# First stage of a four-stage transformer kernel: a tiled product with stationary tokens recast as seven half-size products with stationary weights

## The chip, the cores and the metric

One core of one Trainium2 chip runs the whole program in one launch. The metric is the device time in microseconds. Three runs of the kernel before gave 2706.06, 2711.64 and 2711.44 us (median 2711.44).

## What is computed

The reference stacks eight audio frames into each token (3008 tokens of 2560 numbers), normalises, applies two linear layers with a gate between them, then attention, a feed-forward layer and residual sums. Only the start concerns the change:

```python
x = _rms_norm(x, ln_pre_w)                 # x: 3008 tokens x 2560
h = jnp.einsum('btd,hd->bth', x, w1)       # w1: 1024 x 2560
d = h.shape[-1] // 2
h = jax.nn.silu(h[..., d:]) * h[..., :d]   # 3008 x 512
y = jnp.einsum('btd,od->bto', h, w2)       # the next stage
return _rms_norm(y, ln_post_w)
```

The root-mean-square factor of a token may be put on after the product, since it is one number per token; the kernel does so.

## The kernel before, in words

The program is a chain of five stages: `tok_up`, `tok_down`, `attention`, `attn_out` and `ffn`. Each is one block in which every engine runs its own list, with semaphores between the lists; the next stage begins when all lists of the one before have ended. The change lies in `tok_up` (line 239), with one load in `tok_down` (line 541).

Every product is made in three passes: each operand is split into a high part, which ScalarE (ACT) makes by a copy to the matmul's float type, and a low part, the remainder, which VectorE (DVE) makes by a subtraction. `three_pass` (line 230) then issues high x low, low x high and high x high into the same sum.

`tok_up` works in 24 tiles of 128 tokens. SyncE (SP) loads each tile twice, in four chunks: transposed (`x_t` into `raw`, line 300) for the product, and by rows (`x_rows` into `xs`, line 309) for the sum of squares. ACT makes `x_hi` (L327) and the squares (L336), DVE makes `x_lo` (L366). TensorE (PE) holds the tokens stationary and streams 512 columns of weights: 20 parts of the contraction x 3 passes x 2 halves = 120 matmuls a tile, 2880 in all (L235). All of `w1` lies split in SBUF; its 40 pieces are loaded, multiplied by the norm's weights `fac` and split during the first tile (L203, L213, L222). ACT then applies silu (L345), DVE multiplies the halves (L374), PE turns the result over in four transposes (L415), ACT copies it out (L350) and SP stores it (L294). The next stage loads it by tile (line 541).

GpSimd (POOL) does nothing in this stage. The order on each engine is written out by hand and repeated for every tile; a step of two stages in depth lets the gate of one tile run beside the product of the next.

## Time and profile before

| | us |
|---|---|
| median of three runs | 2711.44 |
| lowest, highest run | 2706.06, 2711.64 |
| span of the profiled execution | 2708.5 |
| last `tok_up` matmul begins to end | about 695 |
| first load of `tok_down` issued | 700.50 |

The profile gives one execution, from its first to its last instruction; its span stands in for its own time, and it lies 2.9 us below the median of the runs. Rows of groups read: line of the kernel, engine, operation, output<-inputs, shape, count, then busy time in us and the mean of one in ns, then the idle time before them and what ended it. PE is TensorE's matmuls, PEld its loads of the stationary operand, SPq the issue of a DMA by SyncE. [...]

### The profile page before, as it was taken

How to read it: one execution, taken by the hardware profiler on the slowest of the kernel's cores; microseconds unless marked ns; L12 is line 12 of the kernel's file. 1: busy time of each engine (PE TensorE's matmuls, PEld its weight loads, DVE VectorE, ACT ScalarE, POOL GpSimd, SP SyncE). 2: the span in 40 equal slices, each digit the busy share in tenths (PEclk: the TensorE clock that was granted, in tenths of full speed). 3: DMA queues.
4: the chain of work that ended last, by engine and by line, in shares of the span. 5: the costliest groups of instructions: out<-in, count | busy, mean ns of one | idle time of the engine just before them, and what ended most of it. 6: DMA issues, size and time to landing. Idle time of an engine off the chain costs nothing. (4 is left out here: it accounts for less than half of the span.)

```text
span 2708.5 us, 47164 instructions
## 1 busy us (share of the span) xinstructions
PE 2569.8 (95%) x15800; PEld 2242.7 (83%) x15800; DVE 1400.3 (52%) x3285; ACT 1108.6 (41%) x3526; POOL 568.0 (21%) x582
## 2 busy tenths in 40 slices
PE   6999999999699997999999999989999999699998
PEld 4888888888577776899999999868888888699998
DVE  5121221222366665799899899841111111777775
ACT  6222222222344444889899899831111110211010
POOL 0000000000011121666666666600000000111110
PEclk9999999999799998999999999989999999899999
DMA  7323233332444543111111111163332222322121
GB/s 238 125 86 127 86 115 98 101 112 89 161 157 153 181 152 114 50 47 42 45 45 41 45 45 41 41 221 102 104 99 93 93 93 70 108 71 71 62 78 47
DMA packets 157346, 260.59 MB, mean 96 GB/s; under 512 B 16432, under 2 KB 92720, under 8 KB 157232
## 3 DMA queue, kind: packets, MB, share of 16 engines
q1 hardware_dynamic: 150048, 233.63, 26.4%
q0 software_dynamic: 7184, 25.69, 2.6%
q8 instruction: 40, 0.66, 0.1%
q14 instruction: 74, 0.61, 0.1%
HBM read 177.49 MB, written 81.79 MB: 96 GB/s over the span
## 5 line engine op out<-in xcount | busy, mean ns | idle before, releaser
L1137 ACT ACTIVATE attn_prob<-attn_prob,attn_bias 94x94 f32<-94x94 f32 x1024 | 367.3, 361 | 58.1 <-DVE attn_bias L1214 58.0
L366 DVE TENSOR_TENSOR up_x_lo<-up_raw,up_x_hi 128x640 fp32r<-128x640 f32 x96 | 79.2, 825 | 474.7 <-ACT up_x_hi L327 474.6
L235 PE MATMUL up_ps_h<-up_w_hi,up_x_lo 128*128 128x512 f32 x960 | 301.5, 396 | 22.1 <-DVE up_w_lo L222 19.1
L235 PE MATMUL up_ps_h<-up_w_lo,up_x_hi 128*128 128x512 f32 x960 | 298.3, 392 | 0.0
L235 PE MATMUL up_ps_h<-up_w_hi,up_x_hi 128*128 128x512 f32 x960 | 298.1, 392 | 0.0
L1346 DVE TENSOR_TENSOR out_x_lo<-out_raw,out_x_hi 128x512 fp32r<-128x512 f32 x96 | 66.5, 693 | 400.0 <-ACT out_x_hi L1331 399.9
L235 PE MATMUL out_ps_h<-out_w_hi,out_x_lo 128*128 128x512 f32 x768 | 238.6, 392 | 11.4 <-DVE out_w_lo L220 10.8
L1331 ACT ACTIVATE out_x_hi<-out_raw 128x512 fp32r<-128x512 f32 x96 | 60.6, 631 | 433.9 <-PE out_ps_h L235 282.7
L1496 POOL TENSOR_TENSOR ffn_res<-shared_h,ffn_bias 128x1024 f32<-128x1024 f32 x24 | 59.7, 2492 | 850.4 <-DMA ffn_bias<-base_b 555.3
L235 PE MATMUL out_ps_h<-out_w_lo,out_x_hi 128*128 128x512 f32 x768 | 237.3, 390 | 0.0
L235 PE MATMUL out_ps_h<-out_w_hi,out_x_hi 128*128 128x512 f32 x768 | 237.2, 390 | 0.0
L1253 POOL TENSOR_TENSOR attn_prob<-attn_prob,attn_share 94x752 f32<-94x752 f32 x128 | 184.3, 1440 | 219.9 <-DVE attn_share L1222 219.9
L235 PEld LDWEIGHTS up_ps_h<-up_w_hi,up_x_lo 128*128 128x128 f32 x960 | 179.0, 189 | 62.1 <-issue 15.7
L235 PEld LDWEIGHTS up_ps_h<-up_w_hi,up_x_hi 128*128 128x128 f32 x960 | 181.5, 189 | 38.6
L235 PEld LDWEIGHTS up_ps_h<-up_w_lo,up_x_hi 128*128 128x128 f32 x960 | 181.4, 189 | 38.4
L327 ACT ACTIVATE up_x_hi<-up_raw 128x640 fp32r<-128x640 f32 x96 | 71.0, 739 | 330.3 <-PE up_ps_h L235 222.5
L1137 ACT ACTIVATION_READ_ACCUMULATOR attn_prob<-attn_prob,attn_bias 94x1 f32 x1024 | 191.6, 187 | 0.0
L235 PEld LDWEIGHTS out_ps_h<-out_w_hi,out_x_lo 128*128 128x128 f32 x768 | 144.0, 188 | 44.1 <-issue 11.3
L235 PEld LDWEIGHTS out_ps_h<-out_w_lo,out_x_hi 128*128 128x128 f32 x768 | 144.8, 188 | 30.2
L235 PEld LDWEIGHTS out_ps_h<-out_w_hi,out_x_hi 128*128 128x128 f32 x768 | 144.5, 188 | 30.0
L235 PE MATMUL ffn_ps_o<-ffn_w_hi,ffn_xt_lo 128*128 128x390 f32 (+1 forms) x576 | 139.8, 351 | 10.2 <-DVE ffn_xt_lo L1584 10.2
L1193 DVE TENSOR_TENSOR attn_prob<-attn_ps_s,attn_mask 94x752 f32<-94x752 f32 x128 | 119.5, 933 | 56.5 <-PE attn_ps_s L1060 56.2
(206 smaller groups left out, 5373.7 us busy)
## 6 DMA issues: line engine op xcount, KB each, us to landing
up_raw<-x_t SPq DMA_DIRECT2D x96, 320.0 KB, 4.4
up_xs<-x_rows SPq DMA_DIRECT2D x96, 320.0 KB, 3.6
out_raw<-o_t SPq DMA_DIRECT2D x96, 256.0 KB, 4.3
o_t<-attn_o_t SPq DMA_DIRECT2D x128, 188.0 KB, 1.9
shared_ring<-wo SPq DMA_DIRECT2D x32, 512.0 KB, 5.2
y<-down_y POOLq DMA_DIRECT2D x24, 512.0 KB, 3.0
out_y<-y SPq DMA_DIRECT2D x24, 512.0 KB, 5.7
h<-out_h SPq DMA_DIRECT2D x24, 512.0 KB, 3.1
```

What stands on the lines that cost most here:

```text
L235: last = nc.tensor.matmul(o, x, w, start=a, stop=b, skip_group_check=onto)
L327: nc.scalar.activation(x_hi[c][:], raw[c][:], ACT.Copy).then_inc(hi_done, 1)
L366: nc.vector.tensor_tensor(x_lo[c][:], raw[c][:], x_hi[c][:], ALU.subtract).then_inc(lo_done, 1)
L1137: last = nc.scalar.activation(prob[u % NPR][0:SEQ, h, part], prob[u % NPR][0:SEQ, h, part], ACT.Exp, bias=bias[u % 2][0:SEQ, n:n + 1], sca ...
L1193: nc.vector.tensor_tensor(p4, ps_s[0:SEQ, :, 0:GT].rearrange("p h (b k) -> p h b k", b=GB), mask[0:SEQ, :].unsqueeze(1).unsqueeze(1).broad ...
L1253: nc.gpsimd.tensor_tensor(p4, p4, share[u % 2][0:SEQ, :].unsqueeze(2).broadcast_to((SEQ, 8, SEQ)), ALU.mult).then_inc(prob_done, 1)
L1331: nc.scalar.activation(x_hi[c][:], raw[c][:], ACT.Copy).then_inc(hi_done, 1)
L1346: nc.vector.tensor_tensor(x_lo[c][:], raw[c][:], x_hi[c][:], ALU.subtract).then_inc(lo_done, 1)
L1496: nc.gpsimd.tensor_tensor(res[u % 3][:], h[u % 3][:], bias[:], ALU.add).then_inc(res_done, 1)
```

## The change

The product is computed transposed: weights stand in the array, tokens stream past, so the outcome comes out with hidden units on the partitions, as the next stage wants it, and the transposes fall away. The 3008 tokens are cut into six chunks (502, 502, 502, 502, 500, 500), which form three pairs of a left and a right half. The 2560 inputs are cut into two halves of ten parts and the 1024 outputs into two halves of four blocks. Each of these 2x2-by-2x2 products is then made by seven products in place of eight: an operand is one block or the sum or difference of two, and each outcome is added to, set in or subtracted from one or two blocks of the result `c_t`, which lies in SBUF.

The work is 7 products x 3 pairs x 10 parts = 210 steps; one step is 4 blocks x 3 passes = 12 matmuls of 502 (or 500) columns, 2520 in all. For a step SP loads one or two pieces of x (257 KB each); where there are two, POOL adds or subtracts them (`both`, L502); ACT makes the high part `t_hi` (L562) and DVE the low part `t_lo` (L664). There are five buffers of each. For every product ten new pieces of the stationary operand are made: SP loads one or two weight pieces through three slots (`w_raw`, L445), ACT scales the one (L533), DVE adds the other (`w_sum`, L620), ACT makes `s_hi` (L544) and DVE `s_lo` (L609). They are made one each at steps 5 to 10 of the third pair of the product before (and at two steps of the second pair), and the last two at the first two steps of the product itself. At steps 6 to 9 DVE folds the outcomes of the group before from PSUM into `c_t`.

During the first four products ACT also squares each piece of x (L577), and DVE or POOL sums the squares. In the fifth product 24 one-column matmuls sum them over the partitions, DVE takes the inverse root, and before each of three groups PE spreads it over the partitions by two matmuls whose outcome ACT copies out at the group's fifth step (L591). The gate runs over 4 x 502 elements at a time (L696, L700, L705).

Cut to its core:

```diff
-def tok_up(nc, d, split, ident):
+TOKC = [(0, 502), (502, 502), (1004, 502), (1506, 502), (2008, 500), (2508, 500)]
+SEVEN = [
+    Product([(0, 0)], [(0, 1), (1, 1)], [(0, 1, SET)], minus_b=True),
+    Product([(1, 0), (1, 1)], [(0, 0)], [(1, 0, SET), (1, 1, FROM)]),
+    Product([(0, 0), (0, 1)], [(1, 1)], [(0, 1, ADD), (0, 0, NEG)]),
+    Product([(1, 1)], [(1, 0), (0, 0)], [(1, 0, ADD), (0, 0, ADD)], minus_b=True),
+    Product([(0, 0), (1, 1)], [(0, 0), (1, 1)], [(0, 0, ADD), (1, 1, ADD)]),
+    Product([(1, 0), (0, 0)], [(0, 0), (0, 1)], [(1, 1, ADD)], minus_a=True),
+    Product([(0, 1), (1, 1)], [(1, 0), (1, 1)], [(0, 0, ADD)], minus_a=True),
+]
+def tok_up(nc, d, ident):
+    KH = KIN // 2
+    PAIR = 3
+    NS, NT, NR, NWR = KH + 2, 5, 6, 3
...
+        def weights_at(s):
+
+            i, pr, kk = place(s)
+            out = []
+            if i == 0 and pr == 0 and kk + 1 < KH:
+                out.append(kk + 1)
+            if i + 1 < NI:
+                if pr == 1 and kk in (2, 6):
+                    out.append((i + 1) * KH + (kk - 2) // 4)
+                if pr == 2 and kk >= 4:
+                    out.append((i + 1) * KH + kk - 2)
+            if i > 0 and pr == 0 and kk < 2:
+                out.append(i * KH + KH - 2 + kk)
...
+            def load_weights(q):
+                p, kk = SEVEN[q // KH], q % KH
+                for k, (mh, kh) in zip(w_of[q], p.a):
+                    old = w_slots.before(k)
+                    if old is not None:
+                        sp.wait_ge(s_lo_done, old + 1)
+                    sp.dma_start(w_raw[w_slots.slot(k)][:],
+                                 d["w1"][:, KH * kh + kk, HID * mh:HID * mh + HID]).then_inc(w_in[w_slots.slot(k)], 16)
+
+            def load_x(s):
+                i, pr, kk = place(s)
+                for k, (kh, nh) in zip(x_of[s], SEVEN[i].b):
+                    old = raws.before(k)
+                    if old is not None:
+                        if is_sum(old):
+                            sp.wait_ge(both_done, nth_sum[old] + 1)
+                        else:
+                            sp.wait_ge(lo_done, old + 1)
+                        if old in squared:
+                            sp.wait_ge(sq_done, squared.index(old) + 1)
+                    sp.dma_start(raw[raws.slot(k)][:, 0:width(pr)],
...
+            nc.gpsimd.memset(zero[:], 0.0).then_inc(zero_set, 1)
+            for s in range(STEPS):
+                i, pr, kk = place(s)
+                w = width(pr)
+                if is_sum(s):
+                    n = nth_sum[s]
+                    for k in x_of[s]:
+                        pool.wait_ge(raw_in[raws.slot(k)], 16 * raws.uses(k))
+                    if n >= 2:
+                        pool.wait_ge(lo_done, sums[n - 2] + 1)
+                    a, b = (raw[raws.slot(k)][:, 0:w] for k in x_of[s])
+                    nc.gpsimd.tensor_tensor(both[n % 2][:, 0:w], a, b, SEVEN[i].op_b).then_inc(both_done, 1)
...
+            def first_piece(q):
+
+                p, kk = SEVEN[q // KH], q % KH
+                k = w_of[q][-1]
+                mh, kh = p.a[-1]
+                act.wait_ge(w_in[w_slots.slot(k)], 16 * w_slots.uses(k))
+                if len(p.a) == 1:
+                    dst, sem = s_hi[q % NS], s_hi_done
+                    free_slot(q)
+                else:
+                    dst, sem = w_one, one_done
+                    n = nth_w_sum[q]
+                    if n > 0:
+                        act.wait_ge(sum_done, n)
+                at = KH * kh + kk
+                nc.scalar.activation(dst[:], w_raw[w_slots.slot(k)][:], ACT.Copy, scale=fac[:, at:at + 1]).then_inc(sem, 1)
+
+            def free_slot(q):
+                if q >= NS:
+                    i, kk = (q - NS) // KH, (q - NS) % KH
...
+            def second_piece(q):
+                if len(SEVEN[q // KH].a) == 2:
+                    act.wait_ge(sum_done, nth_w_sum[q] + 1)
+                    free_slot(q)
+                    nc.scalar.activation(s_hi[q % NS][:], w_sum[:], ACT.Copy).then_inc(s_hi_done, 1)
...
+            def weights_sum(q):
+                p, kk = SEVEN[q // KH], q % KH
+                if len(p.a) == 2:
+                    k = w_of[q][0]
+                    at = KH * p.a[0][1] + kk
+                    dve.wait_ge(w_in[w_slots.slot(k)], 16 * w_slots.uses(k))
+                    dve.wait_ge(one_done, nth_w_sum[q] + 1)
+                    dve.wait_ge(s_lo_done, q)
+                    nc.vector.scalar_tensor_tensor(w_sum[:], w_raw[w_slots.slot(k)][:], fac[:, at:at + 1], w_one[:],
+                                                   ALU.mult, p.op_a).then_inc(sum_done, 1)
...
+            def take(g, m):
+
+                i, pr = g // PAIR, g % PAIR
+                w = width(pr)
+                dve.wait_ge(used, KH * g + KH)
+                src = ps[g % 2][m][:, 0:w]
+                for mh, nh, how in SEVEN[i].into:
+                    c = c_t[:, MB * mh + m, cols(pr, nh)]
+                    if how != SET and how != NEG:
+                        dve.wait_ge(taken, 4 * (g - PAIR) + m + 1)
+                    if how == SET:
+                        ins = nc.vector.tensor_copy(c, src)
+                    elif how == NEG:
+                        ins = nc.vector.tensor_scalar(c, src, -1.0, None, ALU.mult)
+                    elif how == FROM:
+                        ins = nc.vector.tensor_tensor(c, c_t[:, MB * 0 + m, cols(pr, nh)], src, ALU.subtract)
+                    else:
+                        ins = nc.vector.tensor_tensor(c, c, src, ALU.add)
+                ins.then_inc(taken, 1)
...
+                for m in range(MB):
+                    if kk == 0 and g >= 2:
+                        pe.wait_ge(taken, 4 * (g - 2) + m + 1)
+                    if kk == 0 and g == STAT_AT and m == 3:
+                        pe.wait_ge(stat_taken, 1)
+                    if kk == 0 and g in RATE_AT and m >= 2:
+                        pe.wait_ge(rate_taken, 2 * RATE_AT[g][m - 2] + 2)
+                    o = ps[g % 2][m][:, 0:w]
+                    sh, sl = (x[q % NS][:, P * m:P * m + P] for x in (s_hi, s_lo))
+                    nc.tensor.matmul(o, sh, tl, start=(kk == 0), stop=False)
+                    nc.tensor.matmul(o, sl, th, start=False, stop=False)
+                    last = nc.tensor.matmul(o, sh, th, start=False, stop=(kk == KH - 1))
+                last.then_inc(used, 1)
...
-                    sp.dma_start(g_raw[u % 2][:], d["g_t"][t].rearrange("p (j c) -> p j c", j=4)).then_inc(g_in[u % 2], 16)
+                    sp.dma_start(g_raw[u % 2][:], d["g_t"][:, :, bass.ts(t, P)]).then_inc(g_in[u % 2], 16)
...
-    for n, shape in (("wq_pair", (PAIRS, P, 2, 2 * P)), ("wvo", (P, PAIRS, DM)), ("g_t", (TILES, P, HID)),
+    for n, shape in (("wq_pair", (PAIRS, P, 2, 2 * P)), ("wvo", (P, PAIRS, DM)), ("g_t", (P, 4, TOKP)),
```

How the weights reach the engines, on two lists. First SyncE's list of DMAs in `tok_up`. Before, in the first tile, weight pieces go through five buffers, and each waits for the low part made from the buffer's last piece:

```order
L203 DMA up_gt0<-w1 128x512 [waits split_lo_done]
L203 DMA up_gt1<-w1 128x512 [waits split_lo_done]
L203 DMA up_spare0<-w1 128x512 [waits split_lo_done]
L309 DMA up_xs1<-x_rows 128x640
L300 DMA up_raw0<-x_t 128x640 [waits up_lo_done]
L309 DMA up_xs0<-x_rows 128x640 [waits up_sq_done]
```

After, in the last steps of the fifth product (each of its successor's operands is a sum of two pieces):

```order
L459 DMA up_raw2<-x_f 128x500 [waits up_both_done]
L459 DMA up_raw3<-x_f 128x500 [waits up_both_done]
L445 DMA up_w_raw2<-w1 128x512 [waits up_s_lo_done]
L445 DMA up_w_raw0<-w1 128x512 [waits up_s_lo_done]
L459 DMA up_raw4<-x_f 128x500 [waits up_both_done]
L459 DMA up_raw5<-x_f 128x500 [waits up_both_done]
L445 DMA up_w_raw1<-w1 128x512 [waits up_s_lo_done]
L445 DMA up_w_raw2<-w1 128x512 [waits up_s_lo_done]
```

What moved: the weight pieces now come in pairs through three slots, in the middle of the loads of x, and stay there for six steps in a row before each product and two at its start.

Second, VectorE's list. Before, one tile in the steady part:

```order
L366 TENSOR_TENSOR up_x_lo<-up_raw,up_x_hi 128x640 [waits up_link,up_hi_done]
L366 TENSOR_TENSOR up_x_lo<-up_raw,up_x_hi 128x640 [waits up_hi_done] x3
L374 SCALAR_TENSOR_TENSOR up_sil<-up_ps_h,up_r,up_sil 128x512 [waits up_sil_done]
L379 TENSOR_REDUCE up_var<-up_ssq 128x1 [waits up_sq_done]
L380 TENSOR_SCALAR up_var<-up_var 128x1 [waits up_link]
L130 TENSOR_SCALAR up_var<-up_var 128x1 [waits up_link]
```

After, two steps at the end of the fifth product:

```order
L620 SCALAR_TENSOR_TENSOR up_w_sum<-up_w_raw,up_fac,up_w_one 128x512 [waits up_s_lo_done,up_one_done,up_w_in2]
L640 TENSOR_TENSOR up_c_t<-up_c_t,up_ps_0 128x502 [waits up_taken,up_used]
L640 TENSOR_TENSOR up_c_t<-up_c_t,up_ps_0 128x502 [waits up_taken]
L609 TENSOR_TENSOR up_s_lo<-up_w_sum,up_s_hi 128x512 [waits up_s_hi_done]
L664 TENSOR_TENSOR up_t_lo<-up_both,up_t_hi 128x500 [waits up_hi_done]
L620 SCALAR_TENSOR_TENSOR up_w_sum<-up_w_raw,up_fac,up_w_one 128x512 [waits up_s_lo_done,up_one_done,up_w_in1]
```

What moved: between the sum of two weight pieces and its low part now stand two folds of outcomes into `c_t`, and the low part of the next x piece stands behind all of them.

## Rows read from the trace of the kernel before

**Rows 1.** The page: busy time in us by engine, share of the span, instructions.

```profile
PE 2569.8 (95%) x15800; PEld 2242.7 (83%) x15800; DVE 1400.3 (52%) x3285; ACT 1108.6 (41%) x3526; POOL 568.0 (21%) x582
```

**Rows 2.** Busy time in a stretch: us; per engine busy (instructions); clock, DMA share, GB/s.

```profile
300.00:400.00 100.00, 100.00 (x450) 82.75 (x450) 21.45 (x62) 25.75 (x50) 0.00 (x0) 1.00 0.27 88
```

**Rows 3.** Timeline of PE in the first stage: start us, us, engine, line, operation.

```profile
300.50 0.62 PE L235 MATMUL up_ps_h<-up_w_hi,up_x_lo 128*128 128x512 f32 x2
300.95 0.62 PE L235 MATMUL up_ps_h<-up_w_lo,up_x_hi 128*128 128x512 f32 x2
```

**Rows 4.** Timeline of PE in the second stage, matmuls into one PSUM bank.

```profile
760.84 0.34 PE L235 MATMUL down_ps_a<-down_wa_lo,down_xt_hi 128*128 128x384 f32 x1
761.01 0.34 PE L235 MATMUL down_ps_a<-down_wa_hi,down_xt_hi 128*128 128x384 f32 x1
```

**Rows 5.** Instructions of the silu tile: ns min/median/max, first and last start us.

```profile
L345 ACT ACTIVATE up_sil<-up_ps_h,up_r x24: 669/669/690, 63.3 to 695.2; 128x512 f32<-128x512 f32 x24
```

**Rows 6.** Timeline of all engines at the start of the first stage.

```profile
7.06 1.42 DVE L222 SCALAR_TENSOR_TENSOR up_w_lo<-up_sil,up_fac,up_w_hi 128x512 fp32r<-128x512 f32 x2 [0.17 <-ACT up_w_hi L213]
7.83 0.99 SPq L203 DMA_DIRECT2D up_sil<-w  x2
8.62 1.19 PE L235 MATMUL up_ps_h<-up_w_hi,up_x_lo 128*128 128x512 f32 x2 [8.62 <-DVE up_w_lo L222]
10.45 0.72 ACT L213 ACTIVATE up_w_hi<-up_sil,up_fac 128x512 fp32r<-128x512 f32 x1 [0.83 <-DMA up_sil<-w]
```

**Rows 7.** Timeline at the end of the first stage and the start of the second.

```profile
694.55 0.61 PE L235 MATMUL up_ps_h<-up_w_hi,up_x_hi 128*128 128x512 f32 x2
698.04 0.35 SPq L294 DMA_DIRECT2D g_t<-up_gt  x1
700.50 0.34 SPq L541 DMA_DIRECT2D down_g_raw<-g_t  x1
703.41 0.63 ACT L654 ACTIVATE down_g_hi<-down_g_raw 128x512 fp32r<-128x512 f32 x1 [5.39 <-DMA down_g_raw<-g_t]
```

**Rows 8.** Groups by line: ACT's and DVE's prices, then POOL's.

```profile
L213 ACT ACTIVATE up_w_hi<-up_sil,up_fac 128x512 fp32r<-128x512 f32 x16 | 11.2, 722 | 5.7 <-DMA up_sil<-w 5.6
L222 DVE SCALAR_TENSOR_TENSOR up_w_lo<-up_sil,up_fac,up_w_hi 128x512 fp32r<-128x512 f32 x16 | 11.6, 748 | 4.8 <-ACT up_w_hi L213 4.7
L1346 DVE TENSOR_TENSOR out_x_lo<-out_raw,out_x_hi 128x512 fp32r<-128x512 f32 x96 | 66.5, 693 | 400.0 <-ACT out_x_hi L1331 399.9
L732 DVE TENSOR_TENSOR down_xt_lo<-down_ps_x,down_xt_hi 128x512 fp32r<-128x512 f32 x48 | 30.8, 680 | 0.4 <-ACT down_xt_hi L647 0.4
L1240 POOL TENSOR_TENSOR attn_by_sin<-attn_swapped,attn_sin 128x376 f32<-128x376 f32 x128 | 125.9, 984 | 7.4 <-DVE attn_swapped L1173 7.4
L1496 POOL TENSOR_TENSOR ffn_res<-shared_h,ffn_bias 128x1024 f32<-128x1024 f32 x24 | 59.7, 2492 | 850.4 <-DMA ffn_bias<-base_b 555.3 <-DVE ffn_o L1618 295.1
L1156 DVE TENSOR_TENSOR attn_w_lo<-attn_w_raw,attn_w_hi 128x256 fp32r<-128x256 f32 x32 | 54.8, 1714 | 0.0
```

**Rows 9.** Timeline of POOL and DVE in the attention stage.

```profile
1400.51 1.44 POOL L1253 TENSOR_TENSOR attn_prob<-attn_prob,attn_share 94x752 f32<-94x752 f32 x1 [1.64 <-DVE attn_share L1222]
1401.91 0.98 POOL L1240 TENSOR_TENSOR attn_by_sin<-attn_swapped,attn_sin 128x376 f32<-128x376 f32 x1
...
1401.39 1.79 DVE L1156 TENSOR_TENSOR attn_w_lo<-attn_w_raw,attn_w_hi 128x256 fp32r<-128x256 f32 x1
```

**Rows 10.** Busy time in stretches, columns as in rows 2 (PE, PEld, DVE, ACT, POOL).

```profile
10.00:20.00 10.00, 7.90 (x28) 5.72 (x26) 5.99 (x9) 6.99 (x11) 0.00 (x0) 1.00 0.91 297
30.00:40.00 10.00, 7.50 (x26) 5.62 (x25) 7.76 (x11) 6.91 (x11) 0.00 (x0) 0.83 0.80 253
705.00:730.00 25.00, 14.02 (x39) 10.54 (x40) 15.67 (x30) 13.37 (x20) 1.74 (x2) 0.65 0.82 270
```

**Rows 11.** The page's DMA issues: count, KB each, median us to landing.

```profile
up_sil<-w SPq DMA_DIRECT2D x16, 256.0 KB, 4.1
out_raw<-o_t SPq DMA_DIRECT2D x96, 256.0 KB, 4.3
```

More of the change, by code:

```diff
@@ new lines, with __init__ @@
+class Product:
+    def __init__(self, a, b, into, minus_a=False, minus_b=False):
+        self.a, self.b, self.into = a, b, into
+        self.op_a = ALU.subtract if minus_a else ALU.add
+        self.op_b = ALU.subtract if minus_b else ALU.add
+LOW, HIGH = 0, 1
+SET, NEG, ADD, SUB_, FROM = "set", "neg", "add", "sub", "from"
+SEVEN = [
[7 more added lines that the diff above has]
+]
@@ new lines, with __init__, take, slot @@
+class Slots:
+    def __init__(self, n):
+        self.n, self.at = n, []
+    def take(self, owner):
+        self.at.append(owner)
+        return len(self.at) - 1
+    def slot(self, k):
+        return k % self.n
+    def uses(self, k):
+        return k // self.n + 1
+    def before(self, k):
+        return self.at[k - self.n] if k >= self.n else None
+def tok_up(nc, d, ident):
+    KH = KIN // 2
+    PAIR = 3
+    NI = len(SEVEN)
+    STEPS = NI * PAIR * KH
+    MB = 4
+    W = 502
+    NS, NT, NR, NWR = KH + 2, 5, 6, 3
@@ L262, in tok_up @@
-        w1.into([(w_hi[:, n, a], w_lo[:, n, a], fac[:, n:n + 1]) for n, a in halves])
-        PER = 2 * KCH
-        ps_h = [mem.ps(f"ps_h{i}", [P, 2 * HID]) for i in range(2)]
-        ps_t = [mem.ps(f"ps_t{i}", [P, HID]) for i in range(2)]
-        raw_in = mem.sems("raw_in", NCH)
-        xs_in = mem.sems("xs_in", 2)
+        c_t = mem.sb("c_t", [P, 2 * MB, TOK])
+        s_hi = [mem.sb(f"s_hi{i}", [P, HID], F32R) for i in range(NS)]
+        s_lo = [mem.sb(f"s_lo{i}", [P, HID], F32R) for i in range(NS)]
@@ new lines, in tok_up @@
+        t_hi = [mem.sb(f"t_hi{i}", [P, W], F32R) for i in range(NT)]
+        t_lo = [mem.sb(f"t_lo{i}", [P, W], F32R) for i in range(NT)]
+        raw = [mem.sb(f"raw{i}", [P, W]) for i in range(NR)]
+        both = [mem.sb(f"both{i}", [P, W]) for i in range(2)]
+        w_raw = [mem.sb(f"w_raw{i}", [P, HID]) for i in range(NWR)]
+        w_one = mem.sb("w_one", [P, HID])
+        w_sum = mem.sb("w_sum", [P, HID])
+        ssq = mem.sb("ssq", [P, TOK])
+        sq = [mem.sb(f"sq{i}", [P, 4 * SUB]) for i in range(2)]
@@ new lines, in is_sum @@
+        def is_sum(s):
+            return len(SEVEN[place(s)[0]].b) == 2
+        sums = [s for s in range(STEPS) if is_sum(s)]
+        nth_sum = {s: n for n, s in enumerate(sums)}
+        squared = [s for s in range(STEPS) if place(s)[0] < 4]
+        first_in = [s for s in squared if place(s)[2] == 0 and place(s)[0] < 2]
+        adders = [s for s in squared if s not in first_in]
+        by_dve = [s for s in adders if is_sum(s)]
+        by_pool = [s for s in adders if not is_sum(s)]
+        sq_of = {s: n % 2 for n, s in enumerate(adders)}
@@ new lines, in tok_up @@
+        raws = Slots(NR)
+        x_of = {s: [raws.take(s) for _ in SEVEN[place(s)[0]].b] for s in range(STEPS)}
+        w_slots = Slots(NWR)
+        w_of = {q: [w_slots.take(q) for _ in SEVEN[q // KH].a] for q in range(NI * KH)}
+        w_sums = [q for q in range(NI * KH) if len(SEVEN[q // KH].a) == 2]
+        nth_w_sum = {q: n for n, q in enumerate(w_sums)}
+        def weights_at(s):
[10 more added lines that the diff above has]
+                out.append(i * KH + KH - 2 + kk)
+            return out
@@ new lines, in tok_up, with group @@
+        last_of = {}
+        for g in range(NI * PAIR):
+            for mh, nh, how in SEVEN[g // PAIR].into:
+                last_of[(g % PAIR, mh, nh)] = g
+        def group(i, pr):
+            return i * PAIR + pr
+        STAT_AT = group(4, 1)
+        RATE_AT = {group(4, 2): (0, 1), group(5, 0): (2, 3), group(5, 1): (4, 5)}
+        GATE_FIRST, GATE_LAST, VALUE = {}, {}, {}
+        for pr in range(PAIR):
+            GATE_FIRST[KH * group(5, pr + 1) + 0] = 2 * pr
+            GATE_LAST[KH * group(5, pr + 1) + 4] = 2 * pr
+            GATE_FIRST[KH * group(5, pr + 2) + 1] = 2 * pr + 1
+            GATE_LAST[KH * group(5, pr + 2) + 5] = 2 * pr + 1
+            VALUE[KH * group(5, pr + 2) + 8] = 2 * pr + 1
+            if pr < 2:
+                VALUE[KH * group(6, pr + 1) + 9] = 2 * pr
@@ L1702, in build @@
         split = Splitter(nc)
-        tok_up(nc, d, split, ident)
+        tok_up(nc, d, ident)
         shared = Memory(nc, ctx, "shared")
@@ L1785 @@
     arrays = {
[L1786 to L1787 removed]
+        "x_f": x_f,
         "w1": blocks(np.asarray(L0_tok_w1).T),
```

396 lines of the change are left out of this document (253 added, 143 removed).

## The prediction

> **What bounds the kernel now.** I read the page first: PE is busy 95% of the span, DVE 52%, ACT 41%, POOL 21% [rows 1], so no other engine can shorten the time unless it first holds PE up. Then a stretch of the first stage: PE busy all of 100 us at full clock, DVE 21, ACT 26, POOL 0, DMA share 0.27 [rows 2]. The stage is a plain stream of matmuls. Its price is the distance between starts: two matmuls of 512 columns in 0.45 us, 0.2265 each [rows 3]. From the first silu to the last, 23 tiles take 631.9 us, 27.5 a tile [rows 5]; 120 matmuls make 27.2 of it. The first tile is different: it starts at 8.6 and its silu comes at 63.3 [rows 5, 6], about 27 us more than a tile needs, because the weights are loaded and split in it at 250 to 300 GB/s with the DMA engines 80 to 91% busy [rows 10]. The last product ends at 695.2, and the next stage's first load is issued at 700.5 [rows 7]. Everything behind that I take as unchanged but for one load. The account is made against the profile's span of 2708.5; the runs' median, 2711.4, lies 2.9 above it.
>
> **The bare stream.** Matmuls of 384 columns, all into one bank, start 0.173 us apart [rows 4], those of 512 0.2265; so ten columns fewer save 0.004, and three passes in a row into one bank cost nothing extra. 2520 x 0.222 = 560 us. Start: weight and x land, then POOL's sum, ACT's high and DVE's low part; POOL's 1.26 (below) and one load more make it 10.5 instead of 8.6. The 24 + 6 small matmuls: 1. End: four folds of 0.68 and four multiplications of 0.68 in DVE's row, then a store; before, last matmul to next load took 5.3 [rows 7], of which some 2.4 are the store and the block's end after it is issued: 5.4 + 0.7 + 2.4 = 8.5. Bare end: 10.5 + 560 + 1 + 8.5 = 580, that is 120.5 under the 700.5. Without stalls the change would be a large gain; 24 x 4 transposes and the 27 us of the first tile are in that figure.
>
> **What feeds it.** A step of 12 matmuls lasts 2.67 us. Prices: ACT 0.63 for a high part [rows 7], 0.72 with the scale; DVE 0.68 for 502 elements, 0.75 for the scaled form; PSUM as an input changes nothing (0.680 against 0.693) [rows 8]. POOL's addition has no row at 502 elements: between 0.98 (376) and 2.49 (1024), by the straight line 1.26 [rows 8]. An ordinary step costs ACT 1.25, DVE 0.68 to 1.36, POOL 1.26, two loads of 257 KB 1.8 us at 285 GB/s [rows 10]: all below 2.67.
>
> **POOL against DVE.** A DVE subtraction of two SBUF operands, 256 elements, takes 1.79 us in the attention stage [rows 9]: it starts while POOL runs, outlasts two POOL operations and ends 0.3 after the second. Its 32 instances average 1.71, where twice the elements cost 0.69 with POOL idle [rows 8]. So such an operation stands still while POOL works. POOL now works in every step up to the seventh product: 150 sums of x and 57 of squares, 207 x 1.26 = 260 us, and DVE's operations on two SBUF operands are 210 + 57 + 70 + 50 at about 0.7 = 275, with gates 310. Together 570: just inside 560 plus stalls. It decides product 1, first pass: 1.26 + 0.68 (low part of x) + 0.68 (squares) + 0.75 (low weights) = 3.37, less a little overlapped start-up, 3.2 a step: 10 x 0.53 = 5; I add 4 for its other passes, where folds join. Ends: 0 if they share freely, 20 if nothing overlaps. I take **9**.
>
> **The changeovers.** This is the largest term. Before a product whose stationary operands are sums, eight operands are made one a step. The second piece for operand q+1 takes the slot of the first piece of q, so its load is issued only when the low part of q is done. That closes a chain: issue to ACT's start 2.62 (7.83 to 10.45) [rows 6], ACT 0.72, DVE's sum 0.75, ACT's high part 0.63, DVE's low part 0.69, handoffs 0.2: **5.6 us a step where PE needs 2.67**. In four of the eight steps DVE folds two outcomes (1.36) between sum and low part, where only ACT's 0.63 was to be covered: 6.3. SP, ACT and DVE are all in this row: the x loads stand behind the weight loads on SP's queue, `t_hi` behind `s_hi`, `t_lo` behind `s_lo`. So PE starves, although it does not need the weights yet. 4 x 5.6 + 4 x 6.3 = 47.6 against 8 x 2.67 = 21.4: 26.2 too many; four tiles prepared ahead cover 10.7: 15.5 left. Five of six changeovers are of this kind (the product with a single stationary block is made through three slots with ease). The one out of product 1 begins with little prepared: 20. The last three also run on sums of x: fewer tiles ahead, and after the chain the pairs of x must be fetched anew (2.62 + 0.9 + 1.26 + 0.63 + 0.68 = 6.1 before the next tile), so 25 each. 20 + 15 + 75 = **110**. Ends: 5 x 15.5 = 78, or, if a load lands in the 4.1 that weight pieces took beside others [rows 11], 1.5 more for each of 40 links, 170.
>
> **Waits for the factor.** In three groups PE needs the two banks that ACT copies at the group's fifth step, behind five new tiles: a step or so each, **8**; behind them PE then has five tiles ready. The wide gates (2.2 us on DVE) fall where slack is, except in the last changeover, counted above.
>
> **The clock.** Where PE starved in short gaps the granted clock fell now and then: 0.83 over 30 to 40 us, 0.65 over 705 to 730 [rows 10]. [...] I take **5**. [...]
>
> **The next stage** loads `g_t` in rows of 512 B in place of 2 KB. Its first load took 2.9 us [rows 7]; a load of the same size from rows that short takes 4.3 among others [rows 11]: between 0 and 1.4, I take **1.5** with the weights queued behind it; the other 23 are fetched ahead.
>
> **Sum.** 580 + 9 + 110 + 8 + 5 = 712, against 700.5: +11.5, with 1.5 behind it +13. Profiled span 2721.5; on the median 2711.4 + 13 = 2724.4, **2725 us**. A measurement of this kernel tells 0.2% (5.4 us) from no change.
>
> **Rivals.**
> *A, the chain is short and POOL in nobody's way (faster).* If changeovers cost only 15.5 each and DVE isn't held, the stage ends at 580 + 78 + 8 + 2 = 668: -32.5, 2680. For it: 2.62 is the whole of a lone load. Against: [rows 9]. It decides from a mean stall of under some 22 a changeover. Chance 0.22.
> *B, PE-bound throughout.* Loads and splits run ahead, stalls of 20 in all: 600, about 2612. Against: one wait per step on the slot. 0.06.
> *C, loads land late.* 4.1 instead of 2.62 in the chain, since two x pieces are always queued beside: +60, 2785. For it [rows 11]; against: in the chain SP issues the weight first and little is outstanding. 0.14.
> [...] 0.10.
> The forecast's own case (2705 to 2738) has 0.48.
>
> **How the numbers follow.** Faster by over 0.2%: A, B and a fringe of the forecast, 0.30. Same: the lower part of the forecast, 0.12. Slower: the rest of it, C and D, 0.58. Range: from just under A, 2675, to C, 2785; B and a tail beyond C are left out. The likeliest case's own range is 2705 to 2738.
>
> **What would show it.** PE's distance 0.222; PE's idle time in the stage 110 to 140 us, nearly all at the ends of products 1, 2, 4, 5 and 6 and the two or three steps behind each, in steps of 5.5 to 7 us; SP waiting for `s_lo` there; `t_lo` of 0.68 stretched beyond 1.2 where POOL runs; POOL's sum at 1.26; the second stage's first load at about 712. Wrong if: PE starves evenly in all products (then DVE with POOL is the bound), or the changeovers show steps under 4 us, or POOL's sum takes over 1.5.

## The result, and the profile after

The changed kernel takes 2772.33 us (median of 5 runs, 2759.58 to 2777.58), against 2710.53 in the 5 runs of the kernel before beside it: a ratio of 1.0222, 95% interval 1.0205 to 1.0239. The forecast was 2725 with a range of 2675 to 2785. Slower was the likeliest sign, the range holds the time, and the size is 47 us off. The profiled execution is the fastest of the five, 2759.58 us with a span of 2757.9: 49.4 us more than the span before.

Where those 49.4 us lie is read from landmarks, the first start of three groups and the first load of the second stage.

| start, us | before | after | distance |
|---|---|---|---|
| first load of `tok_down` | 700.50 | 717.08 | +16.6 |
| first matmul of `attn_ps_r` | 1083.7 | 1097.7 | +14.0 |
| first matmul of `out_ps_h` | 1773.6 | 1822.7 | +49.1 |
| end of the span | 2708.5 | 2757.9 | +49.4 |

So the account that the prediction gives for the first stage and the loads behind it (+13) comes out within 1 us where the attention stage begins. That closeness is in part luck: the stream of matmuls is 14 us longer than charged and the stalls are 9 shorter (worked out below). **The other 35 us arise inside the attention stage, of which the diff touches no line.** First the page of after: busy time, which answers to [rows 1], and the DMA queues.

```profile
PE 2522.0 (91%) x15404; PEld 2199.7 (80%) x15404; DVE 1695.6 (61%) x3420; ACT 1190.9 (43%) x3618; POOL 873.6 (32%) x791
...
q8 instruction: 108, 1.77, 0.3%
q14 instruction: 102, 0.84, 0.1%
```

The same two rows of the page of before:

```profile
q8 instruction: 40, 0.66, 0.1%
q14 instruction: 74, 0.61, 0.1%
```

DVE gained 295 us of work and POOL 306, and PE has 396 instructions fewer. The rows to stop at are the small ones: queue 8 brings instructions in packets of 16 KB, 40 of them before and 108 now. Then the waits of after in the attention stage, 1115 to 1815 us (total, times, longest in us):

```profile
DVE attn_by_cos L1508 <- PE attn_ps_r L1379: 26.7, 7, 5.2
...
PEld attn_ps_r L1377 <- issue: 24.2, 6, 4.5
POOL attn_by_sin L1576 <- DVE attn_swapped L1509: 24.0, 6, 4.8
PE attn_ps_r L1377 <- issue: 23.1, 6, 4.3
ACT attn_q_a L1446 <- PE attn_ps_l L1379: 20.5, 6, 4.2
```

None of these is among the waits of 10 us and more in the same view of before. "issue" says that PE waited for no semaphore that the profile shows, six times, 23 us. DVE and ACT wait for PE in turn, and POOL for DVE. One of the six in the timeline of PE:

```profile
1439.51 0.87 PE L1420 MATMUL attn_ps_o<-attn_prob_t,attn_v 96*64 96x94 f32 x16
1444.12 0.65 PE L1377 MATMUL attn_ps_r<-kept_qn_hi,attn_w_lo 128*128 128x376 f32 x1 [3.75 <-issue]
```

The six gaps lie at 1265.2, 1355.0, 1444.1, 1533.8, 1624.3 and 1713.1 us, 89 to 91 us apart: once in each turn of this stage's loop, behind its jump back. Busy time in one turn of the loop, before and then after (PE, PEld, DVE, ACT, POOL; clock, DMA share, GB/s):

```profile
1414.60:1497.90 83.30, 81.03 (x834) 76.85 (x836) 74.94 (x149) 75.35 (x310) 54.51 (x49) 1.00 0.13 44
```

```profile
1439.60:1528.70 89.10, 82.63 (x834) 78.39 (x836) 75.47 (x149) 75.43 (x310) 54.09 (x49) 0.98 0.12 43
```

The same instructions, the same traffic, 5.8 us more in this turn. And the DMA queues in one turn, before (1414 to 1498) and after (1350 to 1440):

```profile
q1 hardware_dynamic: 2709, 3.78, 12.9%
q14 instruction: 5, 0.04, 0.2%
```

```profile
q1 hardware_dynamic: 2736, 3.80, 11.8%
q8 instruction: 9, 0.15, 0.7%
q14 instruction: 5, 0.04, 0.2%
```

Before, queue 8 brings nothing in the loop after its first turn. In after it brings nine packets in every turn, and by the trace's DMA records one of them starts inside each of the six stops (at 1262.5, 1352.4, 1441.5, 1531.1, 1621.7 and 1710.5 us), each time 2.6 to 2.7 us before PE goes on. So the stops go with this queue. That queue 8 is PE's follows from its packets, which start about every 256 of PE's records (below).

The first stage itself ends 5 us later than foreseen. Its end, from the timeline (answers to [rows 7]):

```profile
708.90 0.39 PE L753 MATMUL up_ps<-up_t_hi,up_s_hi 128*128 128x500 f32 x1
...
710.75 4.23 SPq L485 DMA_DIRECT2D g_t<-up_c_t  x4
...
717.08 0.64 SPq L877 DMA_DIRECT2D down_g_raw<-g_t  x1
...
720.48 0.63 ACT L990 ACTIVATE down_g_hi<-down_g_raw 128x512 fp32r<-128x512 f32 x1 [21.25 <-DMA down_g_raw<-g_t]
```

The groups of that stage (busy time and mean, then idle time before them):

```profile
L751 PE MATMUL up_ps<-up_t_lo,up_s_hi 128*128 128x502 f32 (+1 forms) x840 | 344.3, 410 | 87.7 <-DVE up_t_lo L664 72.4 <-ACT up_ssq L587 15.2
L502 POOL TENSOR_TENSOR up_both<-up_raw 128x502 f32<-128x502 f32 (+1 forms) x150 | 232.7, 1556 | 282.6 <-DMA up_raw<-x_f 101.5 <-issue 94.1 <-DVE up_t_lo L664 87.0
L664 DVE TENSOR_TENSOR up_t_lo<-up_both,up_t_hi 128x502 fp32r<-128x502 f32 (+1 forms) x150 | 142.8, 953 | 87.8 <-ACT up_t_hi L562 84.2
L533 ACT ACTIVATE up_w_one<-up_w_raw,up_fac 128x512 f32<-128x512 f32 x50 | 35.9, 719 | 75.6 <-DMA up_w_raw<-w 75.6
```

And one link of the chain on which the prediction's largest term rests, in the third pair of the second product: SP issues the raw weights, ACT and DVE make the tile, and the next issue follows.

```profile
178.54 0.33 SPq L445 DMA_DIRECT2D up_w_raw<-w  x1
...
181.31 0.73 ACT L533 ACTIVATE up_w_one<-up_w_raw,up_fac 128x512 f32<-128x512 f32 x1 [2.89 <-DMA up_w_raw<-w]
182.12 0.75 DVE L620 SCALAR_TENSOR_TENSOR up_w_sum<-up_w_raw,up_fac,up_w_one 128x512 f32<-128x512 f32 x1 [3.03 <-ACT up_w_one L533]
...
182.91 0.63 ACT L544 ACTIVATE up_s_hi<-up_w_sum 128x512 fp32r<-128x512 f32 x1 [0.87 <-DVE up_w_sum L620]
...
183.97 0.68 DVE L609 TENSOR_TENSOR up_s_lo<-up_w_sum,up_s_hi 128x512 fp32r<-128x512 f32 x1
```

From 177.82 to 183.97, one low part to the next, are 6.15 us. DVE's two folds (182.79, 183.38) stand between sum and low part, as the prediction's 6.3 has it.

### The profile page after: what moved, and what is told of

The parts are those of the page before. It is cut to its first block and busy times, and to the rows that moved or that the text cites. A ratio compares the mean times of both kernels' runs of the same rounds, so it can differ in the third digit from the quotient of the medians.

```text
span 2757.9 us, 46872 instructions
## 1 busy us (share of the span) xinstructions
PE 2522.0 (91%) x15404; PEld 2199.7 (80%) x15404; DVE 1695.6 (61%) x3420; ACT 1190.9 (43%) x3618; POOL 873.6 (32%) x791
## 5 line engine op out<-in xcount | busy, mean ns | idle before, releaser
L751 PE MATMUL up_ps<-up_t_lo,up_s_hi 128*128 128x502 f32 (+1 forms) x840 | 344.3, 410 | 87.7 <-DVE up_t_lo L664 72.4
L752 PE MATMUL up_ps<-up_t_hi,up_s_lo 128*128 128x502 f32 (+1 forms) x840 | 338.6, 403 | 0.0
L753 PE MATMUL up_ps<-up_t_hi,up_s_hi 128*128 128x502 f32 (+1 forms) x840 | 336.8, 401 | 0.0
L502 POOL TENSOR_TENSOR up_both<-up_raw 128x502 f32<-128x502 f32 (+1 forms) x150 | 232.7, 1556 | 282.6 <-DMA up_raw<-x_f 101.5
L751 PEld LDWEIGHTS up_ps<-up_t_lo,up_s_hi 128*128 128x128 f32 x840 | 165.3, 197 | 134.4 <-DVE up_t_lo L664 73.9
L1589 POOL TENSOR_TENSOR attn_prob<-attn_prob,attn_share 94x752 f32<-94x752 f32 x128 | 184.3, 1440 | 232.9 <-DVE attn_share L1558 232.9
L235 PE MATMUL out_ps_h<-out_w_hi,out_x_lo 128*128 128x512 f32 x768 | 238.2, 392 | 11.6 <-DVE out_w_lo L220 11.2
L664 DVE TENSOR_TENSOR up_t_lo<-up_both,up_t_hi 128x502 fp32r<-128x502 f32 (+1 forms) x150 | 142.8, 953 | 87.8 <-ACT up_t_hi L562 84.2
L753 PEld LDWEIGHTS up_ps<-up_t_hi,up_s_hi 128*128 128x128 f32 x840 | 165.8, 197 | 35.4
L752 PEld LDWEIGHTS up_ps<-up_t_hi,up_s_lo 128*128 128x128 f32 x840 | 165.8, 197 | 33.7 <-issue 0.5
L562 ACT ACTIVATE up_t_hi<-up_both 128x502 fp32r<-128x502 f32 (+1 forms) x150 | 93.4, 622 | 229.8 <-POOL up_both L502 148.8
```

The source lines that it names most:

```text
L235: last = nc.tensor.matmul(o, x, w, start=a, stop=b, skip_group_check=onto)
L502: nc.gpsimd.tensor_tensor(both[n % 2][:, 0:w], a, b, SEVEN[i].op_b).then_inc(both_done, 1)
L562: nc.scalar.activation(t_hi[s % NT][:, 0:w], src, ACT.Copy).then_inc(hi_done, 1)
L664: nc.vector.tensor_tensor(t_lo[s % NT][:, 0:w], src, t_hi[s % NT][:, 0:w], ALU.subtract).then_inc(lo_done, 1)
L751: nc.tensor.matmul(o, sh, tl, start=(kk == 0), stop=False)
L752: nc.tensor.matmul(o, sl, th, start=False, stop=False)
```

## The experiments

Two questions. What makes the attention loop slow, and is the weights' slot what costs the first stage its gain?

To the first, the trace's records give a count of what PE and its sequencer executed. Where the program runs straight on, a packet of queue 8 starts about every 256 records, mostly at counts of 150 to 190 modulo 256 (that is, 150 to 190 places into a block of 256). So a packet of 16 KB holds 256 instructions. One turn of the attention loop has 1751 records, 6.84 blocks. Counted in program order, each loop once, the loop starts at 178 modulo 256 in before and at 81 in after, since the new first stage is written out step by step and is some 3740 instructions longer. The counts may be a few places off; the distances between the starts are exact. **Theory F** says that the loop's instructions come in once and not again only at some starts, namely where it touches seven blocks and not eight. Its rivals: **G**, something that the new stage leaves behind; **L**, the mere length of the program.

To the second, **theory W** is the prediction's chain through three slots, and **rival V** is DVE and POOL standing in each other's way.

### 90 increments of padding in the changed kernel

```diff
+            for _ in range(90):
+                pe.sem_inc(pad_sem, 1)
             pe.wait_ge(ones_set, 1)
```

> The changed kernel with 90 one-instruction semaphore increments put ahead of TensorE's first wait in the first stage, where TensorE waits for the first load until 10.5 us anyway (90 x 51 ns = 4.6 us); nothing else is changed. Theory F (instruction fetch): in the trace TensorE's instruction queue brings 16 KB (256 instructions) each time TensorE's count of instructions passes a place near 150 modulo 256. The attention loop is 1751 instructions long; it starts at 178 modulo 256 in the kernel before and passes 6 such places, and at 81 in the changed kernel, where it passes 7 and the queue fetches 9 blocks in every turn. 90 more instructions put the start at 171: the loop should stay where it is, the fetches of that stage should end after its first turn (108 instruction packets down to about 45), a turn should take 83.3 us instead of 89.7, and the kernel 2759.6 - 35 = 2725 us in a profile. Rival G (something that the new first stage leaves behind, as g_t's order, memory or queues): no change, 2760. Rival L (the longer program as such puts the loop out of reach): no change either, 2760.

2736.54 us (2734.46 to 2738.45), ratio to before 1.0094 (1.0077 to 1.0111). Queue 8 brings 55 packets instead of 108, the waits on issue at `attn_ps_r` are gone, a turn takes 83.3 us, and from the first `attn_ps_r` to the first `out_ps_h` are 690.2 us (before 689.9, after 725.0). The page:

```profile
q8 instruction: 55, 0.90, 0.1%
```

All of the 35 us are back in that stage, and median against median (2772.33 and 2736.54) the padding takes off 35.8. The kernel is 11 us above the expectation because that was counted from the changed kernel's profiled execution, the fastest of its five: here the attention stage begins 10.4 us later (1108.1 against 1097.7). 3.6 of that is the padding, behind which the first matmul starts at 14.85 instead of 11.21; 2.7 is a longer first stage. The other 4.1 lie between the first load of `tok_down` and the attention stage, which took 384.7 us here and 380.6 in the changed kernel's profiled execution, the least of all twelve traces. G and L fall, unless the padding itself did something.

### 128 increments

The same edit with 128.

> The same as the run with 90 increments, but with 128 of them: the attention loop then starts at 209 modulo 256 and still passes 7 places. Theory F: the fetches stay (9 in a turn, about 108 packets), a turn stays at 89 to 90 us, the kernel at 2760 us, though it has more of the same padding. If it were only the extra increments or their delay at the start that mended anything, this run would be mended as well (2725). Rivals G and L: 2760.

2779.17 us, 109 packets of queue 8, and a turn of 90.9 us. The waits between 1115 and 1815 us:

```profile
PE attn_ps_r L1380 <- issue: 29.9, 6, 5.5
```

So 90 mend the loop and 128 don't: neither a delay nor padding as such does it. The first matmul starts at 20.63; 38 more increments cost 5.8 us, 0.15 each. In the trace they also start 0.15 us apart, though each record lasts 0.051: I had priced them by their length and not by their distance.

### Before with 64 increments

The same lines, `range(64)`, ahead of `pe.wait_ge(ident_in, 16)` in the kernel before.

> The kernel before, with 64 increments ahead of TensorE's first wait (64 x 51 ns = 3.3 us, under the first load). Theory F: the start of its attention loop moves from 178 to 242 modulo 256, the loop passes 7 places, the queue fetches 9 blocks a turn (40 packets up to about 100), a turn goes from 83.3 to 89.7 us, and the kernel from 2710 to about 2745 us with a first stage that is untouched. Rivals G and L: nothing moves, 2710.

2747.25 us (2743.24 to 2753.6), ratio 1.0129 (1.0111 to 1.0147). 94 packets of queue 8, and from `attn_ps_r` to `out_ps_h` 729.5 us instead of 689.9, of which PE's waits on issue behind the jump are:

```profile
PE attn_ps_r L1044 <- issue: 24.6, 6, 4.5
```

The old kernel, every product and load of it as it was, becomes 36 us slower by 64 instructions that do nothing. That settles the first question against G and L.

### Four slots for raw weights

```diff
-    NS, NT, NR, NWR = KH + 2, 5, 6, 3
+    NS, NT, NR, NWR = KH + 2, 5, 6, 4
```

> The changed kernel with four slots for raw weights instead of three; nothing else is changed, TensorE's program is the same. Theory W (the chain of the prediction): at the ends of products 1, 2, 4, 5 and 6 a sum of two weight tiles waits for a slot that the tile sum before it frees, so a link is load 2.6 + four operations, 5.2 to 7.7 us, where TensorE needs 2.67. With four slots two links run at once, a link costs 2.7 to 3.5, and the first stage loses 70 us of its changeovers (first load of the second stage at 717 - 70 = 647 us, kernel 2690 in a profile, the attention loop as slow as in the changed kernel). Rival V (VectorE and GpSimd are what the changeovers wait for; the slot only follows them): the links stay above 5 us and the stage gains under 20 us (2740 to 2760).

2686.34 us (2684.56 to 2687.43), ratio 0.9907 (0.9890 to 0.9924): a slot of 2 KB a partition takes 86 us off the changed kernel's median (72 off the span, 2757.9 to 2685.8) and makes it faster than before. The first weight operation, which waited 75.6 us for its loads, in the groups of 0 to 640 us:

```profile
L533 ACT ACTIVATE up_w_one<-up_w_raw,up_fac 128x512 f32<-128x512 f32 x50 | 35.6, 712 | 4.9 <-DMA up_w_raw<-w 4.7
```

The links in the second product's third pair take 4.0 us instead of 6.2, and the last matmul of the stage starts at 627 instead of 709. What remains of a link is no longer the load. Queue 8 still has 108 packets and the attention loop turns in 90 us, as theory F requires of a program that is no instruction longer. W holds; V holds in so far as 4.0 is still above the 2.73 that PE takes for a step. Yet PE no longer starves there: its steps in the second product's third pair take 2.7 us throughout, since enough tiles are ready ahead.

### Four slots and padding of 60 and 30

The edit above, with 60 increments ahead of PE's first wait and 30 behind its last matmul of the stage.

> Four slots for raw weights and the padding together: 60 increments before TensorE's first wait (the run with 90 there started its first matmul 3.6 us late and the one with 128 there 9.4 us late, so one increment costs 0.15 us and 60 of them 9.2, under the 10.5 us of the first load) and 30 behind its last matmul of the first stage (4.6 us, under the 8 us of stores that follow). Theory F and theory W add up: the run with four slots had a span of 2685.8 us and an attention loop that lost 37 us in its turns to fetches; here it should turn in 83.3 us: 2685.8 - 37 = 2649 us of span, 2650 us, faster than both kernels. Rival I (the two are one thing: a stage that ends sooner meets the fetches or the loads elsewhere): the turns stay at 89 us and the kernel at 2686.

2648.67 us (2645.29 to 2653.36), ratio 0.9772 (0.9756 to 0.9789); span 2647.0, where 2649 was expected. The two parts add up. Split so, the padding is free: the first matmul starts at 10.82.

### Three slots, freed at the sum

```diff
-                        sp.wait_ge(s_lo_done, old + 1)
+                        if old in nth_w_sum:
+                            sp.wait_ge(sum_done, nth_w_sum[old] + 1)
+                        else:
+                            sp.wait_ge(s_lo_done, old + 1)
```

> The changed kernel with its three slots, but where a tile of weights is a sum of two, SP loads the next raw tile into its slot once VectorE has made the sum, not once it has made the sum's low half; no padding. Theory W: this takes two of the five steps out of a link (ACT's high half 0.63, VectorE's low half 0.69, with their handoffs about 1.6 us), so the links of 6.2 us in the second product's third pair come down to 4.6, the first stage loses 25 to 45 us and the kernel comes to 2715 to 2735 us in a profile. Rival V (the operations of VectorE and GpSimd set the links): they stay near 6, the kernel at 2750 to 2760.

2700.86 us (2699.55 to 2706.99), ratio 0.9968 (0.9952 to 0.9983). Links of the second product's third pair: 3.9 to 4.7 us, 4.6 expected. The stage gained more than expected, 66 us (last matmul at 643): 1.6 us in each of 5 x 8 links are 64, so the 25 to 45 that I had written were below my own price. No memory at all buys most of what the fourth slot bought.

### All three together

Four slots, freed at the sum, padding of 60 and 30.

> The two edits of the weights' slots together (four slots, freed at the sum) and the padding of 60 and 30. Theory W: with two links at once the slot has little left to cost; the links go from 3.7 to 5 us down to what ACT and VectorE need for a weight tile beside a token tile (about 2.7 to 3.5), 5 to 15 us less than with four slots and padding alone: 2635 to 2645 us. Rival V: the links at four slots already are bound by VectorE and GpSimd, and nothing is left to gain: the same as with four slots and padding, within 3 us.

2646.40 us (2640.98 to 2648.79), ratio 0.9760 (0.9744 to 0.9776): the fastest version of this study, 2.4% faster than before. But against the version without the early free (2648.67) the difference of 2.3 us is inside the spread. The links stay at 4.0 us, so here V's forecast (the same within 3 us) is met: the slot sets them no longer. What V gives as the cause fits the timeline of one link, but no run with four slots took POOL's work away to show it:

```profile
162.88 0.71 ACT L537 ACTIVATE up_w_one<-up_w_raw,up_fac 128x512 f32<-128x512 f32 x1
...
163.05 1.72 POOL L516 TENSOR_TENSOR up_ssq<-up_ssq,up_sq 128x500 f32<-128x500 f32 x1 [2.31 <-ACT up_sq L581]
...
163.67 1.65 DVE L624 SCALAR_TENSOR_TENSOR up_w_sum<-up_w_raw,up_fac,up_w_one 128x512 f32<-128x512 f32 x1
165.24 0.67 DVE L638 COPY up_c_t<-up_ps 128x502 f32<-128x502 f32 x1
165.35 0.63 ACT L548 ACTIVATE up_s_hi<-up_w_sum 128x512 fp32r<-128x512 f32 x1 [1.77 <-DVE up_w_sum L624]
```

DVE's sum of weights starts inside POOL's sum of squares, ends 0.55 us behind it and takes 1.65 us instead of 0.75, and the folds and low parts stand behind it. PE doesn't feel this link (steps of 2.7 us). Of the 124 us that the changed kernel's stage takes beyond a bare stream (below), 35 are left in this version, most of them at the ends of products 4, 5 and 6.

### POOL's sums cut to 16 columns

```diff
-                    nc.gpsimd.tensor_tensor(both[n % 2][:, 0:w], a, b, SEVEN[i].op_b).then_inc(both_done, 1)
+                    nc.gpsimd.tensor_tensor(both[n % 2][:, 0:16], a[:, 0:16], b[:, 0:16], SEVEN[i].op_b).then_inc(both_done, 1)
```

> The changed kernel with three slots, and GpSimd adds only the first 16 columns of each sum of token tiles (the other columns of the sums are left out of the computation: they stay at a constant), so that GpSimd's 1.25 us are gone from 150 steps while all loads, waits and the other engines' work stay. Theory W (the links of the weights bind at the ends of products): TensorE's distance there stays above 5 us in the second product, which has no such sums in its tokens, 6.2 as before; the sums' contention gives back 15 to 40 us elsewhere: kernel 2720 to 2745 us. Rival V (GpSimd holding VectorE up is most of the loss): all links but those of the second product fall under 4 us, the stage loses 60 us or more, 2700 or less. The low halves of the token tiles should take 0.67 to 0.70 us in nearly all steps in place of a mean of 0.95.

The kernel leaves the other columns of the sums out: they keep the constant with which both buffers are filled at the start (that part of the edit isn't shown). 2738.32 us in one run, 21 us less than the changed kernel's profiled execution and 34 less than its median. The links stay near 6 us (5.7 to 6.2 in the second product's third pair, 6.1 to 6.3 in the fifth's), as W has it. The groups of its first stage:

```profile
L668 DVE TENSOR_TENSOR up_t_lo<-up_both,up_t_hi 128x502 fp32r<-128x502 f32 (+1 forms) x150 | 102.0, 680 | 117.6 <-ACT up_t_hi L566 115.9
...
L506 POOL TENSOR_TENSOR up_both<-up_raw 128x16 f32<-128x16 f32 x150 | 67.7, 451 | 417.4 <-DMA up_raw<-x_f 202.3 <-DVE up_t_lo L668 112.5 <-issue 102.4
```

DVE's low part of a sum falls from a mean of 953 ns to 680, on the same columns and inputs, when only POOL's work shrinks: POOL's sums do hold such operations up. The price of POOL's sums in the whole stage is about 22 us with three slots (last matmul ends at 686.8 instead of 709.3), their own shorter time included. That is a difference of single executions: from its first matmul to its last the unchanged stage took 698.1, 700.8 and 693.0 us in the traces of the changed kernel and of its paddings by 90 and 128, and this one 676.0.

### Where exactly the loop fits

Both on the version with all three edits, with less padding: 60 increments ahead of PE's first wait, and in the second run 20 more behind its last matmul of the stage.

> The version with four slots freed at the sum, but with 60 increments in all, all before TensorE's first wait: the attention loop starts at 141 modulo 256. Theory F puts the starts at which the loop passes six places only at 151 to 191 (places near 150, 1751 = 6 x 256 + 215 instructions): here it passes seven, 9 fetches in each turn, turns of 89 to 90 us, 2640 + 38 = about 2680 us. If instead only the rough distance from the kernel before's 178 counted, or padding in general, it would be 2640 to 2650.

2681.40 us, 109 packets, turns of 89.8 us: as theory F has it.

> The same with 20 more increments behind TensorE's last matmul of the first stage: the loop starts at 161 modulo 256. Theory F: six places, no fetches in the loop after its first turn (about 55 instruction packets), turns of 83.3 us, 2640 to 2648 us. So 20 increments that do nothing should take 35 us off. If the bound were a few places off (above 161), it would be 2680 like the run before it.

2700.84 us, 109 packets, turns of 92.0 us. This expectation was wrong, and the 2680 that it gave for a bound a few places off isn't met either. At 161 the packets still come in every turn, and the loop is slower than anywhere else, since PE stops twice a turn, as its timeline shows:

```profile
1281.84 0.68 PE L1385 MATMUL attn_ps_r<-kept_qn_hi,attn_w_lo 128*128 128x376 f32 x1 [3.97 <-issue]
1285.00 0.47 PE L1386 MATMUL attn_ps_r<-kept_qn_lo,attn_w_hi 128*128 128x376 f32 x1 [2.49 <-issue]
```

The starts tried, with what the loop did (a turn is the mean of five):

| loop start, modulo 256 | kernel | packets of queue 8 | a turn, us |
|---|---|---|---|
| 81 | changed | 108 | 89.6 |
| 141 | all three, 60 | 109 | 89.8 |
| 161 | all three, 80 | 109 | 92.0 |
| 171 | changed, 90 | 55 | 83.3 |
| 178 | before | 40 | 83.3 |
| 209 | changed, 128 | 109 | 90.9 |
| 242 | before, 64 | 94 | 89.8 |

A loop of 1751 instructions lies in seven blocks of 256 when it starts in the first 42 places of a block (7 x 256 - 1751 = 41, and the first place), and in eight otherwise. If theory F holds, the table allows one placing of the blocks' edges: above 161, since 161 is slow and 171 isn't, and below 168, since 209 is slow. So an edge is at 162 to 167; that the earliest packets start when the records are at about 150 was my reason for expecting it there, and why they start ahead of the edge isn't shown. At 161 the jump would then land 1 to 6 instructions ahead of an edge, which fits PE's second stop there, of 2.1 to 2.5 us behind the first matmul. The 16 KB are the size of every packet of queue 8, and the 256 instructions are read from the distances between them. That a loop over eight blocks is brought in again in every turn while one over seven isn't is theory F's reading of the table: no run shows where the instructions are kept or how many blocks there is room for. Nor does any run separate whether the nine packets a turn are the eight blocks and one more.

## Why the prediction was right in part and wrong in size

- **The step that failed** is "Everything behind that I take as unchanged but for one load". The diff moves no instruction of the attention stage against another, but it moves their addresses. The loop there started at 178 modulo 256, where queue 8 brings nothing after the first turn, and the change moved it to 81, where nine packets come in every turn: 35.1 us, three quarters of the miss. The term was put at nothing without a reason. The rest is 1 us in the account up to there, and 11.5 where I put the median 2.9 above the span: it lies 14.4 above it, as the profiled execution was the fastest of five.
- **Bare stream, 580**: first matmul at 11.2 (charged 10.5), last matmul to next load 7.8 (8.5): right. The stream between them was mis-sized. Matmuls of 502 and 500 columns start 0.2277 us apart in the mean of 2318 distances at full clock, not 0.222; those of 512 columns before start 0.2271 apart (2535 distances). So ten columns fewer saved nothing, and the straight line from 384 columns to 512 doesn't hold; why isn't shown. 2520 x 0.2277 = 574 in place of 560. A stretch of after in which PE never stops (us; PE busy, matmuls; clock, DMA share, GB/s):

```profile
254.00:309.00 55.00, 55.00 (x243) 1.00 0.56 174
```

- **POOL's sum, 1.26**: 1.556 in the mean. Its shortest is near 1.24, so the straight line was right for an undisturbed sum, but the disturbance works both ways: the 25 sums during which DVE runs nothing on two SBUF operands take 1.25 to 1.29, the other 125 take 1.61 in the mean and up to 3.32. The prediction's own sign of being wrong ("over 1.5") was met here. What that alone cost isn't separated from the next entry.
- **POOL against DVE, 9** (ends 0 and 20): the run with 16 columns puts it at 22. The mechanism was right, the size too small and the place wrong: of the 5 charged to product 1's first pass PE shows 1.4, and the 22 lie in the changeovers. The low parts took 0.95 in the mean in place of 0.68.
- **Changeovers, 110**: the starts of `t_lo` in the trace give 42.5 + 24.2, 45.1 + 25.4, 29.3 + 25.2, 48.5 + 27.4, 50.1 + 36.4 and 52.8 + 36.5 us for a product's third pair and the next one's first; less 2 x 27.3 (twenty bare steps at 0.2277), that is 12, 16, 0, 21, 32 and 35, together 116, where 20, 15, 0, 25, 25 and 25 were charged. The last two also hold a wait for the factor (charged apart, 8) and the wide gate. The chain was right: links of 5.6 to 8.8 us, 6.4 in the mean of the five changeovers with sums, where 5.6 and 6.3 were charged, and two edits of it that touch nothing else gave 66 and 82 us of the stage back. The single entries are off by up to 10.
- **Clock, 5**: granted 0.84 to 0.95 in the changeovers (460 to 509 us: 0.86, PE busy 31.6 of 49). It fell there, but no changeover ran at half clock throughout. No run shows the 5 as a term of its own; what the trace gives in its place is the 22 us that the matmuls at half clock cost, in the next entry.
- **Stalls in sum**: 709.3 - 11.2 - 574 - 1 = 123 against 132 charged. First load at 717.1 against 712: the stream's 14 too few and the stalls' 9 too many make most of these 5, so that the stage's total came out nearly right is luck. PE's idle row shows only 87.7 of it, below the 110 to 140 forecast: 118 of the 2520 matmuls start 0.42 us apart, at the lower of the two clock levels in the trace's records (0.5, the other is 1.0), which costs 22 us more and counts as busy.
- **Next stage, 1.5**: 16.6 at the first load, 14.0 at attention. The first `g_t` load took 3.4 instead of 2.9. From that load to attention this execution took 380.6 us and before 383.2, but the nine other traces with the new layout 383.0 to 388.2, and the kernel before with padding 386.8. So one execution can't tell 1.5 us here; the term stays open.
- **Rival C** names 2785 and lies near the result, but not by its cause: the raw weights reached ACT 2.8 us after their issue in the link above, not 4.1. The links at the end of the sixth product, of up to 8.8 us, are as long as C has them, but C puts its 60 us into this stage, and the first load behind it came only 5 us later than forecast.

So the first stage's loss was real and came from where it was put. And the runs show how thin it was: with each slot freed at the last reader of its raw tile the same seven products are 0.3% faster than before even with the loop off its place, and with a fourth slot and the loop back at its place 2.4%.

## What to carry to other kernels

A long loop's instructions may be brought in again in every turn at some addresses and not at others, as PE's were here: 89.6 to 92.0 us a turn at five starts, 83.3 at two. Before a change elsewhere in the program is judged by the total, look at the instruction rows of the DMA queues and for waits on "issue" behind the loop's jump; if they appear in a stage that wasn't edited, shift the code ahead of the loop and compare again. And where a slot ring feeds a chain, free the slot at the last reader of the raw data, not at the end of the chain, before paying for more slots.

## What the runs showed of the hardware

- Queue 8 brings packets of 16 KB, one about every 256 records of PE where the program runs straight on. For a loop of 1751 instructions it brings nothing after the first turn at two of the seven starts tried (171 and 178) and nine packets in every turn at the five others, which fits seven blocks against eight with an edge at 162 to 167: 6.3 to 7.6 us more on a turn of 83.3, and 8.7 at the start of 161, where PE stops twice. 3.4 to 5.5 us of it are a stop of PE behind the jump; the clock is 0.98 instead of 1.00 in the turn read of the changed kernel.
- A semaphore increment on PE's queue has a record of 0.051 us, but in a row of them they start 0.15 apart.
- Matmuls of 502 and 500 columns start 0.2277 us apart at full clock and those of 512 columns 0.2271: ten columns fewer save nothing.
- DVE's subtraction with two SBUF operands of 502 columns: 0.68 us when POOL adds only 16 columns, 0.95 in the mean and up to 1.80 beside POOL's full sums. POOL's full sum: 1.24 at its shortest, 1.56 in the mean, up to 3.3.
- Queue 14 brings five packets of 8 KB in each turn of the same loop in before and after alike, without a visible stop; whose instructions they are wasn't tried.
